# A four-layer graph network: dense columns that are nodes, and ScalarE's one-hots in the tensor pass

## The chip, the cores and the metric

One core of a Trainium2 chip runs the whole network as one program. Time is device microseconds (us) of that core. Engines are called PE (TensorE; PEld its weight loads), DVE (VectorE), ACT (ScalarE), POOL (GpSimd) and SP (SyncE).

## The reference

A graph of 6,250 nodes with 128 features and 100,000 edges. Sources are uniform; the destination is floor(6250 × u²), with the edges sorted by destination, so early nodes have very many edges and late ones few. Four layers run over the same edges, each added to x and normalised:

```python
dst = minimum((6250 * uniform(100000) ** 2.0).astype(int32), 99999); sort src, dst by dst
# layer 0, tensor product
w = silu(edge_attr_10 @ W_fc1 / sqrt(10)) @ W_fc2 / sqrt(100)      # per edge, 10 -> 100 -> 128
agg = segment_sum(concat(w1*y0[src]*ea0, w4*dot(y1[src], ea1), ..., w3*y1[src]*ea0), dst)   # 256 wide
# layer 1, gate and GRU
att = sigmoid(x[src] @ W_att[:d] + x[dst] @ W_att[d:] + b_att)
agg = segment_sum((x[src] @ W_msg + b_msg) * att, dst)
# layer 2, twice: the first four edges of each node, sorted by value, weighted
# layer 3, four SAGE layers, 128 -> 256 -> 256 -> 256 -> 128
mean = segment_sum(z[src], dst) / maximum(count(dst), 1);  z = relu(bn(mean @ Wl.T + bl + z @ Wr.T))
```

## The kernel before

**Edges, tiles, groups.** The sorted edges are cut into tiles of 128 (784 with the padding) and groups of four tiles (196). A pass over *cold* edges gathers the source rows of each tile from a table in DRAM by an indirect DMA that GpSimd issues (L1124, L1333, L1664, some 1.0 us each), makes a one-hot of each edge's place in its group's 128-node window, and TensorE multiplies rows by one-hot and sums the group (L1203, L1452, L1751). VectorE adds the group's sum onto the output at the window's base.

**Hot edges.** Where many edges share a destination, gathers are spared: a *dense* matrix of counts (source by column) is multiplied by the table, 49 blocks of 128 sources. It lies in DRAM as `dense` (49, 128, 3840) in f16. Before the change a column is a place in a narrow *window* of up to 30 nodes: 147 windows cover tiles 0 to 535, one after the other in the columns (`EDGES`), with a base node each (`hot_bases`). After the products VectorE adds each window's columns onto the output at its base (L1847 in the SAGE passes), and in the one-output SAGE passes copies 1/count from node order to window order. The gate pass uses the first 1,792 columns (376 tiles, 94 groups, so 102 cold groups), the two-output SAGE passes 2,304 columns (105 hot groups, 91 cold), the one-output ones 3,840 (134 hot, 62 cold). Columns are worked through in two halves (`supers`) of 49 block steps each.

**Building the counts.** `LateBuild` makes them while other passes gather: for each tile VectorE writes a one-hot of the source's low seven bits and one of the key (source block and place in the window), TensorE multiplies the two and sums a window's tiles in PSUM (L2461), and ScalarE evicts each window (L2479) to its fixed columns in a stage of 256, which SP stores. The first 69 windows are built beside the tensor pass, the rest beside the two sort phases. Tile t of the build is done in the turns of the groups of the pass beside it.

**Prep** (11 to 26 us) makes on VectorE, for every edge, its place in the group's window (`rel`), its key in the dense window, and `far.missed`: 1 where an edge of a dense tile does not lie in its dense window though `rel` is below 128. From the maxima of places over all edges comes one flag:

```python
most = max(max place over its window's width + 128, max rel of dense tiles + 64, max rel of all)
far.any = most > 127.5        # in effect
```

**Far edges.** After each of the six passes `far_pass` (L2006) covers the edges that no window holds. Every engine reads the flag and branches over two loops if it is 0 (L2043 and after): one over 48 windows of 128 nodes, one over the pass's hot groups, in which only the missed edges (`far.missed`) count; the tensor pass has only the first. A turn of a loop is this, on all five engines, and SP starts a turn only when the one before is `done`:

```python
            if eng.If(far.any):
                for w in 1..WINDOWS-1: body(w, first group of the window, w * WIN, False)
                if not tensor: for g in 0..hot_groups-1: body(g + WINDOWS, g, bases[g + 1], True)
```

SP loads 4 × 128 source indices; GpSimd issues four gathers; VectorE makes the one-hots (in the gate pass the slots' operands too, and ScalarE the sigmoids; in the tensor pass the products of the edges); TensorE sums them, twelve 128-column bf16 products for each output of a SAGE pass (rows split in three parts), f32 products in the others; VectorE scales and adds onto the output.

**Tensor pass.** In each group's turn VectorE makes the 512-column f32 one-hot (L1225, is_equal of `iota` and `rel`), the build's one-hots and the products of the edges; ScalarE makes silu and three or four scalings of the gathered rows (L1154) and evicts windows; the hidden layer and two sets of sums are on TensorE.

**Gate pass.** 98 dense steps, one in each of the first 98 cold groups: TensorE makes the block's gate logits (L1424), ScalarE the sigmoids, VectorE the products with the counts (L1503), TensorE the sums. x at the dense columns is taken window by window with the windows' bases. Beside each of the first 94 cold groups one hot group's slot places (the first four edges of a node, for the sort) are worked in, in one pair of small operations.

## Time and profile before

| | |
|---|---|
| time, median of 3 runs | 4,715.51 us (4,713.63 to 4,729.36) |
| the profiled execution | 4,711.36 us, span 4,709.5 us |
| PE busy | 3,546.9 us, 75% (weight loads 2,502.4, 53%) |
| DVE busy | 2,819.4 us, 60% |
| ACT busy | 1,252.7 us, 27% |
| POOL busy | 3,057.2 us, 65% |
| mean granted TensorE clock | 0.858 of full speed |

The stages, in us from the span's start: prep 11 to 26; the first table 30 to 90; tensor pass 94 to 1,183; gate pass 1,272 to 1,895.5; its far pass and the GRU to 1,966; the two sort phases 2,020 to 2,287 and 2,322 to 2,588; four SAGE passes, 2,664.7 to 3,064.9 (one output), 3,165.4 to 3,656.6 and 3,733.2 to 4,223.9 (two outputs), 4,284.5 to 4,669.8 (one output); the end at 4,709.5. Shares of busy time over the whole span mix these; read each stage by itself, in the views that cut the span.

### The profile page before, as it was taken

Reading aid. Unit: us, or ns where it says so; the run is one execution under the profiler, and the core shown is the slowest. Engines: PE = TensorE matmul, PEld = TensorE weight load, DVE = VectorE, ACT = ScalarE, POOL = GpSimd, SP = SyncE. Lnnn points to the kernel's source line nnn. Section 1 sums busy time; section 2 is a strip of 40 time slices with the busy share of each in tenths; the row PEclk is TensorE's granted clock in tenths of the full one; section 3 lists DMA queues with packets and bytes.
Section 4 is the critical chain, followed back from the end, with each engine's and each line's share of the span. In section 5 each row is a group of like instructions: output and inputs, shape, how many; then the busy total and the mean of one; then the engine's idle time right before and its main releaser. Section 6 shows DMA issues by size and latency. Waiting matters only on the chain. (4 is left out here: it accounts for less than half of the span.)

```text
span 4709.5 us, 73302 instructions
## 1 busy us (share of the span) xinstructions
PE 3546.9 (75%) x24179; PEld 2502.4 (53%) x24180; DVE 2819.4 (60%) x8637; ACT 1252.7 (27%) x2796; POOL 3057.2 (65%) x2999
## 2 busy tenths in 40 slices
PE   3788887777777777556445598679998699967894
PEld 2666666666644544333222464447766576755552
DVE  4898888887466666677677534354444535354334
ACT  2333344444244343334333200020000200002112
POOL 3777777777277576367477575537776577746663
PEclk7899999998899898765555799889999899988996
DMA  5222333334233343033333586438886488856872
GB/s 194 66 69 64 94 93 93 91 92 140 73 99 100 81 102 78 18 83 105 90 102 82 197 261 199 149 116 267 265 256 198 164 262 264 261 179 216 247 225 81
DMA packets 432943, 684.60 MB, mean 145 GB/s; under 512 B 66971, under 2 KB 306501, under 8 KB 431801
## 3 DMA queue, kind: packets, MB, share of 16 engines
q1 hardware_dynamic: 311992, 385.14, 25.5%
q0 software_dynamic: 120576, 294.77, 22.7%
q8 instruction: 198, 3.24, 0.3%
q14 instruction: 177, 1.44, 0.1%
HBM read 577.20 MB, written 102.45 MB: 144 GB/s over the span
## 5 line engine op out<-in xcount | busy, mean ns | idle before, releaser
L1664 POOL DMA_INDIRECT pass_rows<-table_sage,src_idx x1216 | 1175.8, 967 | 476.7 <-issue 350.3
L1124 POOL DMA_INDIRECT pass_rows<-table_tensor,src_idx x784 | 834.4, 1064 | 246.8 <-issue 236.8
L1725 PE MATMUL pass_dense_ps<-x 128*128 128x512 f16 (+3 forms) x3528 | 605.8, 327 | 31.8 <-DMA x<-table_sage 30.7
L1333 POOL DMA_INDIRECT pass_rows<-table_gate,src_idx x406 | 433.7, 1068 | 202.3 <-issue 118.2
L1725 PE MATMUL pass_dense_ps<-rb 128*128 128x512 f16 (+1 forms) x2352 | 508.7, 373 | 27.4 <-DMA rb<-table_sage 25.2
L2528 POOL DMA_INDIRECT sort_rows<-table_sort,slot_idx x392 | 396.5, 1012 | 182.1 <-issue 162.3
L1751 PE MATMUL pass_sums_ps<-pass_hot,pass_rows 128*128 128x128 bf16 x5856 | 394.7, 224 | 85.9 <-issue 85.9
L1725 PEld LDWEIGHTS pass_dense_ps<-x 128*128 128x128 bf16 x3528 | 314.4, 98 | 266.6 <-DMA x<-table_sage 31.9
L1751 PEld LDWEIGHTS pass_sums_ps<-pass_hot,pass_rows 128*128 128x128 bf16 x5856 | 367.3, 101 | 108.2 <-issue 92.3
L1786 DVE TENSOR_TENSOR pass_scaled_sums<-pass_sums_ps,rc 128x128 f32<-128x128 f32 x364 | 88.9, 285 | 479.4 <-PE pass_sums_ps L1751 471.6
L1725 PEld LDWEIGHTS pass_dense_ps<-rb 128*128 128x128 bf16 x2352 | 229.2, 100 | 263.6 <-DMA rb<-table_sage 26.3
L1154 ACT ACTIVATE pass_y_ea<-pass_rows,rd 128x128 f32<-128x128 f32 x784 | 250.0, 391 | 405.8 <-DMA pass_rows<-table_tensor,src_idx 405.7
L2461 PE MATMUL sort_counts_ps<-sort_hot_key,sort_hot_low 128*128 128x512 bf16 (+4 forms) x502 | 190.8, 519 | 194.2 <-DVE sort_hot_key L2447 150.5
L1203 PE MATMUL pass_sums_ps<-pass_hot,pass_prod_a 128*128 128x128 f32 x1568 | 234.9, 297 | 131.8 <-DVE pass_prod_b L1015 131.0
L1203 PEld LDWEIGHTS pass_sums_ps<-pass_hot,pass_prod_a 128*128 128x128 f32 x1568 | 209.7, 206 | 186.7 <-issue 177.8
L2461 PE MATMUL pass_counts_ps<-rc 128*128 128x512 bf16 (+8 forms) x1039 | 238.1, 355 | 88.5 <-ACT re L2479 88.5
L1424 PE MATMUL pass_dense_ps<-pass_weighted,rd 128*128 128x512 f32 (+1 forms) x392 | 191.8, 616 | 113.2 <-DVE pass_weighted L1503 110.7
L1786 DVE TENSOR_TENSOR rb<-pass_sums_ps,rc 128x128 f32<-128x128 f32 x124 | 36.0, 290 | 350.6 <-PE pass_sums_ps L1751 334.1
L1203 PE MATMUL pass_sums_ps<-pass_hot,pass_prod_b 128*128 128x128 f32 x1568 | 228.9, 294 | 0.0
L1182 PE MATMUL pass_weight_ps<-fc,pass_hidden 100*128 100x128 f32 x1576 | 221.5, 286 | 1.5 <-ACT pass_hidden L1141 1.0
L1203 PEld LDWEIGHTS pass_sums_ps<-pass_hot,pass_prod_b 128*128 128x128 f32 x1568 | 212.8, 211 | 0.0
L2461 PEld LDWEIGHTS sort_counts_ps<-sort_hot_key,sort_hot_low 128*128 128x128 bf16 x502 | 52.9, 124 | 293.8 <-issue 192.5
(351 smaller groups left out, 6758.1 us busy)
## 6 DMA issues: line engine op xcount, KB each, us to landing
rb<-dense SPq DMA_DIRECT2D x196, 480.0 KB
x<-dense SPq DMA_DIRECT2D x196, 288.0 KB
x<-table_sage SPq DMA_DIRECT2D x196, 192.0 KB
dense<-re SPq DMA_DIRECT2D x11, 3136.0 KB, 13.7
pass_counts<-dense SPq DMA_DIRECT2D x98, 224.0 KB
pass_rows<-table_sage,src_idx POOLq DMA_INDIRECT x1216
rb<-table_sage SPq DMA_DIRECT2D x196, 96.0 KB
table_sage<-x SPq DMA_DIRECT2D x24, 768.0 KB
```

The lines of the kernel that those rows point to most:

```text
L1124: nc.gpsimd.indirect_dma_start(rows[:, h, t, :], None, table, bass.IndirectOffsetOnAxis(ap=idx[:, at:at + 1], axis=0)).then_inc(gathered[h ...
L1154: ins = nc.scalar.activation(y_ea0[:, r, t, :], rows[:, h, t, :], ACT.Copy, scale=cols(extra["edge_attr"], (q * GROUP_TILES + t) * 4, 1))
L1182: ins = nc.tensor.matmul(weight_ps[:, r, t * P:(t + 1) * P], hidden[:, r, t * P:(t + 1) * P], extra["w_fc2"], start=True, stop=True)
L1203: ins = nc.tensor.matmul(sums[:, r, a * WIN:(a + 1) * WIN], prod[:, r, t, :], hot[:, r, t, :], start=(t == 0), stop=(t == GROUP_TILES - 1))
L1333: nc.gpsimd.indirect_dma_start(rows[:, h, t, :], None, table, bass.IndirectOffsetOnAxis(ap=idx[:, at:at + 1], axis=0)).then_inc(gathered[h ...
L1424: ins = nc.tensor.matmul(dense_ps[:, at:to], messages[:, k, 0:P], weighted[:, n % 2, at:to], start=(b == 0), stop=(b == BLOCKS - 1))
L1664: nc.gpsimd.indirect_dma_start(rows[:, h, t, :], None, table, bass.IndirectOffsetOnAxis(ap=idx[:, at:at + 1], axis=0)).then_inc(gathered[h ...
L1725: ins = nc.tensor.matmul(dense_ps[:, at:to], table_ring[:, k, from_table:from_table + P], counts_ring[:, k, at - first:to - first], start= ...
L1751: ins = nc.tensor.matmul(sums[:, r, a * P:(a + 1) * P], rows[:, h, t, at:at + P], hot[:, r, t, :], start=(t == 0 and part == 0), stop=(t = ...
L1786: ins = nc.vector.tensor_tensor(scaled_sums[:, a, :], sums[:, r, a * P:(a + 1) * P], cols(inv_count, start, WIN), ALU.mult)
L2461: ins = self.nc.tensor.matmul(self.counts[:, at:at + wide], self.hot_low[:, (t // G) % 2, t % G, :], self.hot_key[:, r, at:at + wide], sta ...
L2528: nc.gpsimd.indirect_dma_start(rows[:, b, j, :], None, table, bass.IndirectOffsetOnAxis(ap=slot_idx[:, at:at + 1], axis=0)).then_inc(gathe ...
```

## The change

**Columns as nodes.** A dense column is now a node. The near share (tiles 0 to 443, 111 groups) has 2,048 columns for nodes 0 to 2,047; the late share (tiles 444 to 551) has 1,184 for nodes 1,980 to 3,163. Each share is an array of its own. Windows remain as units of the build (126 near and 54 late ones, 180 for 147), and neighbours may overlap: the base of a window is worked out in prep on the chip, as the least of where its tiles' edges begin and the farthest that the windows before it let it begin, each at most its width less one on from the one before, and not below the share's first node. An edge outside its window is missed. The maximum that sets `far.any` is now that of `far.missed` × 128 and of `rel`.

**Build.** The last column of a window may also be the first of the next: TensorE adds to the next window's counts what stands at its first column in the stage (one more product of 49 columns for each window, `same` the identity), and ScalarE evicts at an offset read from a register; keys are ordered place by block. Stages that hold no whole window before them are cleared on ScalarE first. There are eleven stores of the near share for seven, and seven of the late one for eight. Count tiles built beside the tensor pass are 444 for 376, and beside the sorts 42 and 66 for 86 and 74.

**Passes.** The gate pass has 85 cold groups for 102 and 2,048 columns for 1,792: 98 steps now fall in 83 groups, so 15 groups have two; x at the columns is one product of 512 for each bank, with no bases; the 111 hot groups' slots go beside 85 cold ones, so 26 of these have a third unit. Its messages are added in two operations of 1,024 columns. The two-output SAGE passes have 2,048 columns for 2,304 and 85 cold groups for 91. The one-output ones have 2,048 and then 1,184 for 3,840, and 58 cold groups for 62; the windows' adds and the copies of 1/count are gone, one scaling and one add of 2,048 or 1,184 columns stand in their place.

**Tensor pass.** ScalarE makes the one-hots: |rel − iota| per tile (four operations), and then Relu(1 − that) over the group's 512 columns, one group ahead. VectorE's is_equal is gone.

**Sizes.** `far_pass` runs over 111 hot groups in the gate and the two-output SAGE passes and 138 in the one-output ones, if it runs.

The diff, cut to its core:

```diff
-    return 2 * math.ceil((nodes * (1 + 3.5 / math.sqrt(P * (end - first))) + 1) / 2)
...
-NARROW = 30
...
+    return 2 * math.ceil((nodes * (1 + 3.5 / math.sqrt(P * (end - first))) + 2) / 2)
...
+def windows_of(first, end, narrow):
+
+
+    best = {first: (0, [])}
+    for to in range(first + 1, end + 1):
+        best[to] = min((best[a][0] + room_for(a, to) * (to - a + 2) + 50, best[a][1] + [to])
+                       for a in range(max(first, to - MOST_TILES), to) if a in best and room_for(a, to) <= narrow)
+    ends = best[end][1]
+    return ends, [room_for(a, b) for a, b in zip([first] + ends, ends)]
...
+HOT_TILES, DENSE_TILES = 444, 552
...
+NEAR_NODES, LATE_FROM, LATE_TO = 2048, 1980, 3164
+LATE_COLS = LATE_TO - LATE_FROM
+NEAR_ENDS, NEAR_WIDTHS = windows_of(0, HOT_TILES, 30)
+LATE_ENDS, LATE_WIDTHS = windows_of(HOT_TILES, DENSE_TILES, 34)
+HOT_CUTS, WIDTHS = [0] + NEAR_ENDS + LATE_ENDS, NEAR_WIDTHS + LATE_WIDTHS
+GATE_WINDOWS, DENSE_WINDOWS = len(NEAR_WIDTHS), len(WIDTHS)
+NEAR_RUNS = runs_of(range(GATE_WINDOWS), NEAR_NODES)
+LATE_RUNS = runs_of(range(GATE_WINDOWS, DENSE_WINDOWS), LATE_TO)
+LATE_PARTS = ((0, len(LATE_RUNS) // 2), (len(LATE_RUNS) // 2, len(LATE_RUNS)))
+
+SHARES = ((0, HOT_TILES, 0, NEAR_NODES, range(GATE_WINDOWS), NEAR_RUNS),
+          (HOT_TILES, DENSE_TILES, LATE_FROM, LATE_TO, range(GATE_WINDOWS, DENSE_WINDOWS), LATE_RUNS))
+APART = 1 << 15
...
+SUPER_COLS = NEAR_NODES // SUPERS
...
+def window_limits():
+
+
+    rooms, least = [], []
+    for share, (_, _, node, end_node, windows, runs) in enumerate(SHARES):
+        last = runs[-1][0]
+        before = list(itertools.accumulate((WIDTHS[w] - 1 for w in windows), initial=0))
+        reaching = [end_node - STAGE_COLS - max(before[last - windows[0]] - at, 0) for at in before[:-1]]
+        assert reaching[0] <= node
+        rooms += [share * APART + at for at in before[:-1]]
+        least += [max(node, at) for at in reaching]
+    return rooms, least
...
+            def one_hots(q):
+
+
+                if q >= 2:
+                    act.wait_ge(summed, q - 1)
+                    act.wait_ge(hot_made, q - 1)
+                for t in range(GROUP_TILES):
+                    ins = nc.scalar.activation(apart[:, q % 2, t, :], iota[:], ACT.Abs, scale=-1.0,
+                                               bias=cols(rel, q * GROUP_TILES + t, 1))
+                ins.then_inc(apart_made, 1)
+                act.wait_ge(apart_made, q + 1)
+                nc.scalar.activation(hot[:, q % 2, :, :], apart[:, q % 2, :, :], ACT.Relu, scale=-1.0,
+                                     bias=extra["ones"]).then_inc(hot_made, 1)
...
+                    if q + 1 < GROUPS:
+                        one_hots(q + 1)
...
-                nc.vector.tensor_tensor(hot[:, r, :, :], iota[:].unsqueeze(1).broadcast_to([P, GROUP_TILES, WIN]),
-                                        cols(rel, q * GROUP_TILES, GROUP_TILES).unsqueeze(2).broadcast_to([P, GROUP_TILES, WIN]),
-                                        ALU.is_equal).then_inc(hot_made, 1)
...
+    steps_in = spread_over([1] * STEPS, COLD_GROUPS - 2) + [[], []]
+    last_group = [next(j for j in range(COLD_GROUPS) if BLOCKS * (u + 1) - 1 in steps_in[j]) for u in range(SUPERS)]
+    own_in = [[i for i in range(BLOCKS) if 1 + i * (COLD_GROUPS - 2) // BLOCKS == j] for j in range(COLD_GROUPS)]
+    single = [j for j in range(COLD_GROUPS) if len(steps_in[j]) < 2]
+    apart = {single[k * len(single) // len(UNPAIRED)]: g for k, g in enumerate(UNPAIRED)}
...
-                starts = []
-                for part in in_parts(supers[u], 8):
-                    starts = load_bases(PE_E, hot_bases, part[0], len(part))
-                    for w, start in zip(part, starts):
-                        first, end = EDGES[w] - u * SUPER_COLS, EDGES[w + 1] - u * SUPER_COLS
-                        bank = min(end, (first // 512 + 1) * 512)
-                        ins = nc.tensor.matmul(gate_ps[:, first:bank], extra["w_dst"], cols(x, start, bank - first),
-                                               start=True, stop=True)
-                        if bank < end:
-                            ins = nc.tensor.matmul(gate_ps[:, bank:end], extra["w_dst"],
-                                                   cols(x, start + (bank - first), end - bank), start=True, stop=True)
+                for at in range(0, SUPER_COLS, 512):
+                    ins = nc.tensor.matmul(gate_ps[:, at:at + 512], extra["w_dst"], cols(x, u * SUPER_COLS + at, 512),
+                                           start=True, stop=True)
...
+                for c, g in enumerate(beside(j)):
+                    nc.vector.tensor_tensor(hot_narrow[:, r, c, :, :], iota_half[:, 0:HOT_WIN].unsqueeze(1).broadcast_to([P, G, HOT_WIN]),
+                                            hot_rel_half[:, g * G:(g + 1) * G].unsqueeze(2).broadcast_to([P, G, HOT_WIN]),
                                             ALU.is_equal)
...
+                into = agg[:, u * SUPER_COLS:(u + 1) * SUPER_COLS]
+                nc.vector.tensor_tensor(into, into, kept if u == 0 else dense_ps[:, 0:SUPER_COLS], ALU.add).then_inc(dense_added, 1)
+                dve.wait_ge(dense_added, u + 1)
...
+                        for at in range(0, nodes, 512):
+                            to = min(at + 512, nodes)
+                            ins = nc.tensor.matmul(dense_ps[:, a * most_cols + at:a * most_cols + to],
+                                                   table_ring[:, k, from_table:from_table + P], counts_ring[:, k, at:to],
+                                                   start=(b == 0 and part == 0), stop=(b == BLOCKS - 1 and part == PARTS - 1))
                 ins.then_inc(stepped, 1)
...
-                    ins = nc.vector.tensor_copy(inv_dense[:, first:end], cols(inv_count, start, end - first))
-                ins.then_inc(spread, 1)
...
+                    into = aggs[a][:, node:node + nodes]
+                    nc.vector.tensor_tensor(into, into, kept[:, a * most_cols:a * most_cols + nodes],
+                                            ALU.add).then_inc(dense_added, 1)
+                    last_add[a] = (dense_added, u * A + a + 1)
...
+            after(nc.vector.tensor_tensor(under, hot_base, hot_room, ALU.subtract))
+            for share, (first, end, node, _, _, _) in enumerate(SHARES):
+                nc.vector.tensor_tensor(repeated[:, first + MOST_TILES:end], dst[:, first + MOST_TILES:end],
+                                        dst[:, first:end - MOST_TILES], ALU.is_equal)
+                ins = nc.vector.tensor_scalar(least_of[0][:, first:end], under[:, first:end], float(node - share * APART), None,
+                                              ALU.min)
+            after(ins)
+
+            reach, now = 1, 0
+            while reach < DENSE_TILES:
+                nc.vector.tensor_copy(least_of[1 - now][:, 0:reach], least_of[now][:, 0:reach])
+                after(nc.vector.tensor_tensor(least_of[1 - now][:, reach:], least_of[now][:, reach:],
+                                              least_of[now][:, 0:DENSE_TILES - reach], ALU.min))
+                reach, now = 2 * reach, 1 - now
+            after(nc.vector.tensor_tensor(under, least_of[now][:], hot_room, ALU.add))
+            after(nc.vector.tensor_tensor(based, under, hot_least, ALU.max))
...
+            after(nc.vector.tensor_tensor(place, dst[:, 0:DENSE_TILES], based, ALU.subtract))
...
+            after(nc.vector.tensor_tensor(over, place, hot_width, ALU.subtract))
...
+            after(nc.vector.tensor_tensor(least_of[0][:], over, under, ALU.max))
+            for first, end, _, node, _, _ in SHARES:
+                ins = nc.vector.scalar_tensor_tensor(least_of[1][:, first:end], dst[:, first:end], float(-node),
+                                                     least_of[0][:, first:end], ALU.add, ALU.max)
+            after(ins)
+
+            after(nc.vector.scalar_tensor_tensor(over, repeated, -1.0, least_of[1][:], ALU.add, ALU.max))
+            after(nc.vector.scalar_tensor_tensor(inside, over, -0.5, close, ALU.is_le, ALU.mult))
...
+            after(nc.vector.tensor_tensor(far.missed[:], near, inside, ALU.subtract))
...
+            after(nc.vector.reduce_max(most_missed[:], far.missed[:], mybir.AxisListType.X))
+            after(nc.vector.scalar_tensor_tensor(most[:], most_missed[:], float(WIN), most_rel[:], ALU.mult, ALU.max))
...
+        if ends and w > self.windows[0]:
+
+            stage = self.staged(self.run_of(w - 1) % len(self.stages))
+            offset = self.position(PE_E, HOT_CUTS[w], STAGE_COLS - 1)
+            self.nc.tensor.matmul(self.counts[:, 0:BLOCKS], self.same,
+                                  stage[:, :, bass.ds(offset, 1)].rearrange("p b d -> p (b d)"),
+                                  start=False, stop=False, skip_group_check=True)
...
+        stage = self.staged(q % n)
+        if w == first and self.empties(q):
+            self.nc.scalar.activation(stage, self.iota[:, 0:STAGE_COLS].unsqueeze(1).broadcast_to([P, BLOCKS, STAGE_COLS]),
+                                      ACT.Copy, scale=0.0).then_inc(self.emptied, 1)
+            act.wait_ge(self.emptied, sum(map(self.empties, range(self.part[0], q + 1))))
+        if w > self.first:
+            act.wait_ge(self.evicted, w - self.first)
+        at = self.position(ACT_E, HOT_CUTS[w], STAGE_COLS - wide) if w > first else 0
+        self.nc.scalar.activation(stage[:, :, bass.ds(at, wide)],
+                                  self.counts[:, 0:BLOCKS * wide].rearrange("p (d b) -> p b d", b=BLOCKS),
                                   ACT.Copy).then_inc(self.evicted, 1)
...
+                if len(aggs) == 2:
+                    hot_tiles, supers = HOT_TILES, [(dense[0], u * SUPER_COLS, SUPER_COLS, u * SUPER_COLS) for u in range(SUPERS)]
+                else:
+                    hot_tiles, supers = DENSE_TILES, [(dense[0], 0, NEAR_NODES, 0), (dense[1], 0, LATE_COLS, LATE_FROM)]
+                sage_pass(nc, gathers, f"pass3{k}", tab, width, hot_tiles, supers, src_idx, rel, iota_half, bases, room, aggs, own, C)
+                far_edges(f"pass3{k}_far", "sum", tab, width, hot_tiles // GROUP_TILES, aggs, inv_count=C)
...
+    o["hot_width"] = np.repeat(np.asarray(WIDTHS, f32) - 1, np.diff(HOT_CUTS))[None, :]
+    rooms, least = window_limits()
+    o["hot_room"], o["hot_least"] = (np.repeat(np.asarray(v, f32), np.diff(HOT_CUTS))[None, :] for v in (rooms, least))
```

## Rows read from the trace of the kernel before

**Rows 1.** Stretches by stage: start:end, length, busy us by engine, clock, DMA

```profile
94.00:1183.10 1089.10, 860.25 (x5949) 701.08 (x5949) 924.44 (x2626) 434.26 (x1051) 834.37 (x784) 0.93 0.33 89
1272.00:1895.50 623.50, 449.33 (x2532) 306.88 (x2532) 396.05 (x1177) 239.29 (x608) 433.68 (x406) 0.88 0.36 90
...
2664.70:3064.90 400.20, 330.00 (x2214) 200.19 (x2214) 147.63 (x581) 17.99 (x49) 240.20 (x246) 0.90 0.69 214
3165.40:3656.60 491.20, 462.18 (x4340) 332.03 (x4340) 213.03 (x819) 43.01 (x98) 348.18 (x362) 0.97 0.77 244
...
4284.50:4669.80 385.30, 317.03 (x2116) 188.61 (x2116) 139.35 (x532) 42.99 (x98) 237.41 (x246) 0.90 0.69 214
```

**Rows 2.** Groups of instructions, whole span: busy us, mean ns, idle before and releasers

```profile
L1664 POOL DMA_INDIRECT pass_rows<-table_sage,src_idx x1216 | 1175.8, 967 | 476.7 <-issue 350.3 <-PE pass_sums_ps L1751 104.6 <-POOLq L201 21.7
L1124 POOL DMA_INDIRECT pass_rows<-table_tensor,src_idx x784 | 834.4, 1064 | 246.8 <-issue 236.8 <-PE pass_sums_ps L1203 5.7 <-POOLq L201 4.3
L1725 PE MATMUL pass_dense_ps<-x 128*128 128x512 f16 (+3 forms) x3528 | 605.8, 327 | 31.8 <-DMA x<-table_sage 30.7 <-DVE x L1833 1.1
L1725 PE MATMUL pass_dense_ps<-rb 128*128 128x512 f16 (+1 forms) x2352 | 508.7, 373 | 27.4 <-DMA rb<-table_sage 25.2 <-DVE pass_kept L1833 2.2
L1333 POOL DMA_INDIRECT pass_rows<-table_gate,src_idx x406 | 433.7, 1068 | 202.3 <-issue 118.2 <-PE pass_sums_ps L1452 44.5 <-POOLq L201 39.6
...
L1751 PE MATMUL pass_sums_ps<-pass_hot,pass_rows 128*128 128x128 bf16 x5856 | 394.7, 224 | 85.9 <-issue 85.9
...
L1225 DVE TENSOR_TENSOR pass_hot<-iota,rel 128x512 f32<-128x512 f32 x196 | 133.4, 681 | 4.9 <-issue 4.8
...
L1503 DVE TENSOR_TENSOR pass_weighted<-pass_counts,pass_gate_ps 128x896 f32<-128x896 f16 x98 | 105.8, 1079 | 32.1 <-issue 16.4 <-ACT pass_gate_ps L1349 15.6
...
L2479 ACT ACTIVATE re<-pass_counts_ps 128x1470 f16<-128x1470 f32 (+7 forms) x69 | 84.8, 1228 | 137.3 <-PE pass_counts_ps L2461 116.1 <-DMA dense<-re 21.1
```

**Rows 3.** Waits in the first SAGE pass (2664.7 to 3064.9): us, times, longest

```profile
PE pass_own_ps L1707 <- DVE re L1803: 37.4, 6, 12.0
...
PE pass_sums_ps L1751 <- issue: 18.3, 5, 10.5
```

**Rows 4.** Groups of instructions again, VectorE in the SAGE passes

```profile
L1786 DVE TENSOR_TENSOR pass_scaled_sums<-pass_sums_ps,rc 128x128 f32<-128x128 f32 x364 | 88.9, 285 | 479.4 <-PE pass_sums_ps L1751 471.6 <-issue 7.3
...
L1847 DVE TENSOR_TENSOR ra<-ra,pass_kept 128x26 f32 (+9 forms) x294 | 55.0, 187 | 76.0 <-issue 38.2 <-DVE ra L1847 1.3 <-DVE ra L1806 0.3
```

**Rows 5.** Line 2044, sequencers: duration ns min/median/max, first and last start

```profile
L2044 SPq TENSOR_LOAD <-far_any x6: 275/278/466, 1183.6 to 4670.3; - x6
...
L2044 SPq COMPARE_BRANCH  x6: 50/50/50, 1184.4 to 4670.9; - x6
...
L2044 PEldq COMPARE_BRANCH  x6: 200/285/359, 1184.5 to 4671.1; - x6
```

**Rows 6.** DMA issues: times, KB each, median us to landing

```profile
sort_rows<-table_sort,slot_idx POOLq DMA_INDIRECT x392, 2.6
...
sage_early<-in_a_enc SPq DMA_DIRECT2D x1, 64.0 KB, 1.8
```

**Rows 7.** Timeline of the tensor pass around 707 us

```profile
706.22 0.94 POOL L1124 DMA_INDIRECT pass_rows<-table_tensor,src_idx  x1 [0.30 <-issue]
...
708.78 0.98 ACT L1154 ACTIVATE pass_y_ea<-pass_rows,rd 128x128 f32<-128x128 f32 x3 [2.83 <-DMA pass_rows<-table_tensor,src_idx]
```

**Rows 8.** Timeline of TensorE at the gate pass's start

```profile
1292.92 3.36 PE L1424 MATMUL pass_dense_ps<-pass_weighted,rd 128*128 128x512 f32 x4 [3.94 <-DVE pass_weighted L1503]
1296.07 1.20 PE L1445 MATMUL pass_sums_ps<-pass_hot_sig,pass_rows 128*128 128x128 f32 x8
...
1298.40 1.67 PE L1424 MATMUL pass_dense_ps<-pass_weighted,rd 128*128 128x512 f32 x4
```

**Rows 9.** Page, DMA queues of the instruction fetch: packets, MB, share

```profile
q8 instruction: 198, 3.24, 0.3%
q14 instruction: 177, 1.44, 0.1%
```

493 lines of the change are left out of this document (234 added, 259 removed).

## The prediction

> **What bounds the kernel now.** I first read the table of stages [rows 1]. Of each I asked which engine never rests. In the tensor pass it is GpSimd: 784 indirect gathers of 1.064 us, with 0.30 us between two of them that no releaser explains [rows 2], are 784 × 1.37 = 1,071 of 1,089 us. It waited for TensorE only 5.7 us. The gate pass takes longer than its 406 gathers (434 of 623.5 us); there GpSimd waits 44.5 us for TensorE [rows 2], and the loop runs over ScalarE's gates, VectorE's products and TensorE. In the four SAGE passes TensorE is the bound: busy 462 of 491 us with two outputs, 330 of 400 and 317 of 385 us with one. The one-output passes lose the rest where TensorE waits for VectorE's own term (37.4 us in the first) or for something unnamed (18.3 us), in gaps up to 12 us [rows 3]; VectorE is then adding (or copying) windows at 187 ns each, after register loads ("issue", 38.2 us) [rows 4].
>
> One stage hardly appears: the far edges. Six times each engine reads `far_any` and branches past the loops, a load of about 0.3 us and a branch of 0.05 (TensorE's 0.29) [rows 5]. Nothing of line 2043 onward runs but that: the flag is 0.
>
> **The flag after the change.** This decides the case, and it follows from the inputs and the new constants, not from a price. The late share has tiles 444 to 551. Its columns must start at node 1980, so the change clamps the base of its first window to 1980, however late its edges start. The next window may begin at most width − 1 further on. `windows_of` gives the first late windows two tiles and a width of 26, of which 25 places are used: 1980 to 2004, 2005 to 2029, 2030 to 2054. But the expected node at tile 444 is 6,250 × (444 × 128 / 100,000)² = 2,018.7, and two tiles there hold about 18 nodes. The first window holds its edges only if tile 444 starts at or before some 1,986. The fraction 0.568 of 100,000 draws has a deviation of 0.0016, times 2 × 6,250 × 0.568 that is 11 nodes: 1,986 is three deviations away. With the seed of the inputs tile 444 starts at node 2001. Tile 445 then holds nodes 2008 to 2019 against a limit of 2004. Following the new code's bases through all 552 tiles, 298 edges of tiles 444, 445, 447 and 449 lie outside their window; from tile 450 on the bases have caught up, and the near share misses none. Each is marked in `far.missed`, the maximum becomes 1 × 128, and `far.any` is set. Before the change no edge misses (the greatest place is one under its width), in agreement with [rows 5].
>
> **What the flag costs.** All six far stages then run their loops, which cover the missed edges and so keep the sum whole. The loop over windows has 48 turns; all but the tensor pass's add one turn for each hot group: 111, or 138 in the one-output SAGE passes. That is 48 (tensor), 159 (gate), 2 × 159 and 2 × 186 (SAGE): 897 turns. Nothing in a turn is double-buffered: SP waits for `done` of the turn before. One turn, in chain:
> - the index load: a load of 64 KB took 1.8 us, a gather 2.6 from its issue on [rows 6]; I take 2.0.
> - four gathers on GpSimd: 4 × (0.967 + 0.305) = 5.1 us [rows 2].
> - the last one's landing: GpSimd's issue ended at 706.22 + 0.94 = 707.16, ScalarE began on the rows at 708.78 [rows 7]: 1.6 us.
> - TensorE after some 8 us of rest. Four 512-column products took 3.36 us after 3.94 us of idleness and 1.67 us when it had been busy [rows 8], a factor of two, the two levels of its clock. A bf16 product is 394.7 / 5,856 = 0.067 us at the high one [rows 2]; twelve (one output) take 1.6 us at the low one, 24 take 3.2. Eight f32 ones (2 × 0.9 us for each four in [rows 8]) take 3.6.
> - VectorE's scaling and adding, 0.29 us each [rows 4]: 0.7 us, 1.1 with two outputs. In the gate also four sigmoids on ScalarE (1.2, as three operations take 0.98 in [rows 7]) and a 512-column product (0.7, as the one-hot's 0.681 in [rows 2]); in the tensor pass some 2.9 of products, which is what VectorE's 924 / 196 = 4.7 us for each group [rows 1] leaves when the one-hot and the counts' one-hots are off.
> - handovers, four to six at 0.1: 0.4 to 0.6.
>
> Sums: SAGE with one output 2.0 + 5.1 + 1.6 + 1.6 + 0.7 + 0.4 = 11.4; two outputs 13.4; gate 2.0 + 5.1 + 1.6 + 1.2 + 0.7 + 3.6 + 0.6 + 0.5 = 15.3; tensor 16.2. The one-hots, the slot operands and the tensor pass's hidden layer are made while the gathers run (under 5 us against 8.7), so they cost nothing; if they did not fit, each turn would grow by the excess. Total: 372 × 11.4 + 318 × 13.4 + 159 × 15.3 + 48 × 16.2 = 4,241 + 4,261 + 2,433 + 778 = 11,713 us.
> Bounds: with TensorE at the high level throughout, 1,180 us less; with a landing of 2.6 instead of 1.6 (the gather's whole time, [rows 6]), 900 more.
>
> **The rest of the change, against the profiled 4,711.4 us** (span 4,709.5; the median of the runs shown is 4,715.5, 0.1% more).
> - SAGE, two outputs: 98 steps of 3 × 2,048 columns in place of 3 × 2,304 take 606 / 2 × 1/9 = 34 us off TensorE, six groups fewer 6 × 1.56 = 9. The last groups get dense steps too, so its idle time falls a little; GpSimd's 338 × 1.27 + start and end = 440 is then nearly the bound. 491 becomes 446: −45, twice.
> - SAGE, one output: (2,048 + 1,184) / 3,840 leaves 84% of 255 us (−40), four groups fewer −4. The 147 copies and 147 adds per pass become two scalings and two adds of over 1,000 columns, so most of the 56 us of waits in [rows 3] goes. 400 becomes 312 and 385 becomes 305, near GpSimd's 230 × 1.27 = 292. Together −168.
> - Tensor pass: VectorE loses 196 × 0.68 = 133 us [rows 2], but GpSimd sets the pace. ScalarE gains four 128-column operations (1.3 us by [rows 7]) and one of 512 (some 0.6), 1.9 × 196 = 370, and 57 evictions of 1.2 (L2479 in [rows 2]): 434 + 370 + 70 = 874 of 1,089 us, hidden behind the gathers. Matmuls of the counts stay (1,064 for 1,039, and 125 small ones). 0, between −20 (a less busy VectorE beside the gathers) and +60 (TensorE waits at 126 window ends in place of 69).
> - Gate pass: 17 groups fewer × 5.6 ((623.5 − 52) / 102, the 52 an estimate for start, window products and end) = −96; 1/7 more columns in 98 products of 1.079 us [rows 2] +15; 15 groups with two steps at 2.5 (a product and the sigmoids it waits for) +38, and 26 with a third slot unit at 2.4 (seven small operations and a register load) +62; the 138 window products and 69 adds go, −35. −16, between −60 and +30.
> - Prep: some 25 more dependent operations on 552 columns at about 0.7 (the 512-column 0.681): +20. Sort: 52 fewer tiles of counts to build, −8, an estimate, as GpSimd's gathers pace those stages too.
>
> Sum −261: 4,450 us without the loops. With them 4,450 + 11,713 = 16,163, said as 16,160 us.
>
> **Rivals.**
> 1. *The flag stays 0* (I misread a base or the clamp). Then the time is the sum above, 4,450, and this is the side on which it ends faster; it needs that no one of 100,000 edges lies outside its window. For it speaks only that the loops did not run before. Against it stands the arithmetic. 0.11.
> 2. *Every turn fetches its code again.* Each turn jumps back on all five engines. The page's instruction queues moved 3.24 + 1.44 = 4.68 MB for 73,302 instructions, 64 bytes each [rows 9]: the loops that ran before were not fetched twice. But their bodies are other ones, and the one branch over them took TensorE 285 ns against 50 for SP [rows 5]. One fetch of 2.0 us on the chain of each turn would add 897 × 2.0 = 1,800: 18,000 us. 0.07.
> The Trainium skill (Runtime: NRT & Kernel Launch, Instruction fetch mechanics) says that a taken branch whose target isn't in the present window of two pages makes the engine fetch it before it goes on; by that these short bodies would be spared, and the forecast stands, and if they straddle pages it is this rival. The bytes of [rows 9] agree with the first reading.
> 3. *Cheaper turns*: TensorE stays at the high level and handovers vanish: 11,713 − 1,180 − 450 → 14,500 us. 0.05, inside the range.
>
> **Numbers.** 0.75 for the forecast, 0.05, 0.07 and 0.11 for the rivals, 0.02 for something else (of which half within the 0.3% that a measurement of this kernel can tell from no change). Slower 0.88, same 0.01, faster 0.11. The range runs from rival 3 with 900 us to spare, 13,600, to rival 2 with the longer landing, 18,900. It leaves out mainly rival 1; if that held, its own range would be 4,370 to 4,560.
>
> **What would show it.** Right: the far lines (L2043 onward before the change) with hundreds of gathers each, 897 × 4 = 3,588 gathers more, turns of 11 to 16 us, TensorE's clock at 0.5 there, and SAGE passes of about 446 and 310 us beside them. Wrong: six branches as in [rows 5] and a span under 4,600; or turns whose longest wait is none of the five above.

## The result, and the profile after

The changed kernel takes 16,751.2 us (median of 4 runs, 16,737.3 to 16,757.8) against 4,720.7 of the kernel before on the same chip: a ratio of 3.548 (3.540 to 3.555). The profiled execution has a span of 16,755.9 us. The forecast was 16,160, in a range of 13,600 to 18,900.

Stretches by stage, as in [rows 1] (start:end, length, busy us of PE, PEld, DVE, ACT and POOL, clock, DMA share, GB/s); every second one of these lines is a far pass, which [rows 5] showed as a branch:

```profile
114.40:1435.30 1320.90, 871.43 (x6099) 715.28 (x6099) 818.02 (x2515) 869.90 (x2090) 801.17 (x784) 0.86 0.42 83
1437.70:2243.80 806.10, 370.30 (x1248) 269.12 (x1248) 234.58 (x672) 89.98 (x240) 181.03 (x192) 0.54 0.07 17
2328.90:2856.20 527.30, 405.00 (x2230) 247.57 (x2230) 384.03 (x1111) 230.24 (x540) 367.89 (x338) 0.93 0.42 104
2856.80:5526.80 2670.00, 934.09 (x2862) 467.61 (x2862) 548.25 (x1751) 182.09 (x636) 599.96 (x636) 0.50 0.08 16
6340.20:6642.70 302.50, 279.71 (x2019) 172.47 (x2019) 101.98 (x277) 18.02 (x49) 226.79 (x230) 0.97 0.82 252
6645.00:8788.80 2143.80, 271.77 (x2232) 222.72 (x2232) 422.28 (x1116) 0.00 (x0) 702.90 (x744) 0.50 0.14 34
8889.10:9330.40 441.30, 417.87 (x3608) 277.87 (x3608) 170.30 (x532) 42.97 (x98) 327.68 (x338) 0.98 0.81 254
9332.80:11503.80 2171.00, 435.85 (x3816) 393.91 (x3816) 424.86 (x1272) 0.00 (x0) 600.90 (x636) 0.54 0.21 58
...
14257.70:14561.80 304.10, 270.18 (x1921) 161.11 (x1921) 93.65 (x228) 43.01 (x98) 228.13 (x230) 0.98 0.79 240
14564.10:16716.20 2152.10, 271.78 (x2232) 222.71 (x2232) 422.29 (x1116) 0.00 (x0) 714.24 (x744) 0.50 0.13 34
```

(In the order of the lines: tensor pass, its far pass, gate pass, its far pass, first SAGE pass and its far pass, second and its far pass, fourth and its far pass.) The flag is set. The six far passes, with the third SAGE pass's 2,179 us, are 806 + 2,670 + 2,144 + 2,171 + 2,179 + 2,152 = 12,122 us. In them the clock is 0.50 to 0.54, the lower of the two levels nearly throughout, and no engine is busy for half of a stretch. Without them 16,756 - 12,122 = 4,634 us remain.

The gathers of the far loops, line by line of the code (duration min/median/max, first and last start):

```profile
L2114 POOL DMA_INDIRECT pass_far_rows<-table_sage,pass_far_idx x2760: 940/946/1192, 6647.7 to 16711.2; - x198
L2114 POOL DMA_INDIRECT pass_far_rows<-table_gate,pass_far_idx x636: 938/944/999, 2861.0 to 5516.6; - x159
L2114 POOL DMA_INDIRECT pass_far_rows<-table_tensor,pass_far_idx x192: 938/944/952, 1440.5 to 2234.0; - x192
```

2,760 + 636 + 192 = 3,588, which is four for each of 897 turns: as forecast, to one.

One turn of the first SAGE far pass, from the add that ends the turn before to the one that ends this:

```profile
7001.99 0.29 DVE L2245 TENSOR_TENSOR ra<-ra,pass_far_scaled_sums 128x128 f32 x1
...
7005.02 0.94 POOL L2114 DMA_INDIRECT pass_far_rows<-table_sage,pass_far_idx  x1 [6.83 <-DMA pass_far_idx<-in_src]
...
7008.77 0.95 POOL L2114 DMA_INDIRECT pass_far_rows<-table_sage,pass_far_idx  x1 [0.30 <-issue]
...
7011.52 1.46 PE L2168 MATMUL pass_far_sums_ps<-pass_far_hot,pass_far_rows 128*128 128x128 bf16 x12 [10.09 <-DMA pass_far_rows<-table_sage,pass_far_idx]
7013.12 0.29 DVE L2238 TENSOR_TENSOR pass_far_scaled_sums<-pass_far_sums_ps,rc 128x128 f32<-128x128 f32 x1 [8.19 <-PE pass_far_sums_ps L2168]
7013.54 0.29 DVE L2245 TENSOR_TENSOR ra<-ra,pass_far_scaled_sums 128x128 f32 x1
```

It is one serial chain: nothing of the next turn has begun before this one ends, and VectorE's one-hots (not shown) lie under the index load. 2.74 us pass from the end of the add (7,002.28) to the first gather, for handing over, loading 2 KB of indices (4 × 128 of 4 bytes) and handing over again; four gathers take 4.70; 1.80 until TensorE has the last rows; its twelve products 1.46 at the low clock; 0.14, and 0.71 for scaling and adding. Together 11.55 us, the time from one add to the next; the passes' mean is 2,143.8 / 186 = 11.53.

Next the instruction fetch, with 140,036 instructions run (packets, MB, share):

```profile
q8 instruction: 182, 2.98, 0.1%
q14 instruction: 169, 1.38, 0.0%
```

The changed kernel with the flag clear (experiment 1), which skips every loop and runs 68,170 instructions, fetched the same 182 and 169 packets, 4.36 MB. That settles rival 2: no turn fetched its code again. The Trainium skill (Runtime: NRT & Kernel Launch, Instruction fetch mechanics) lets a taken branch force a fetch only where its target lies outside the present window of two pages; the bytes agree.

**What went the other way.** The prediction had the tensor pass at 1,089 us still. It took 1,321. Waits there (us, times, longest):

```profile
POOL pass_rows L1141 <- PE pass_sums_ps L1237: 272.9, 42, 36.5
...
ACT re L2550 <- DMA dense<-re: 202.1, 9, 24.8
...
ACT re L2544 <- DMA dense<-re: 26.4, 1, 26.4
```

ScalarE waits 202.1 + 26.4 = 228 us for the store of the stage of counts to land; before it was 21.1 us in four waits. The issues of this store, before and after (KB, median us from issue to landing, over the whole span):

```profile
dense<-re SPq DMA_DIRECT2D x11, 3136.0 KB, 13.7
```

```profile
dense<-re SPq DMA_DIRECT2D x14, 3136.0 KB, 27.2
```

The same 3,136 KB in one store, at twice the time. One such wait on ScalarE, and on GpSimd at the same time:

```profile
772.46 0.72 ACT L1171 ACTIVATE pass_hot<-rd,ones 128x512 f32<-128x512 f32 x1
797.96 1.07 ACT L2550 ACTIVATE re<-pass_counts_ps 128x1078 f16<-128x1078 f32 x1 [24.78 <-DMA dense<-re]
```

```profile
783.61 0.94 POOL L1141 DMA_INDIRECT pass_rows<-table_tensor,src_idx  x1 [0.31 <-issue]
807.27 0.94 POOL L1141 DMA_INDIRECT pass_rows<-table_tensor,src_idx  x1 [22.71 <-PE pass_sums_ps L1237]
```

ScalarE stands before the first eviction of a run. Behind it in its queue are the hidden layer and the scaled rows of the next group; without them TensorE makes no sums and no buffer of rows comes free. GpSimd, which sets the pace, ends its last free gather at 784.6 us and then stands for 22.7.

### The profile page after: what moved, and what is told of

Same layout as the page of the kernel before. It is cut to its first block and busy times, and to the rows that moved or that the text cites. A ratio compares the mean times of both kernels' runs of the same rounds, so it can differ in the third digit from the quotient of the medians.

```text
span 16755.9 us, 140036 instructions
## 1 busy us (share of the span) xinstructions
PE 6005.4 (36%) x38254; PEld 4255.4 (25%) x38255; DVE 4988.6 (30%) x14480; ACT 1959.6 (12%) x4622; POOL 6297.6 (38%) x6439
## 5 line engine op out<-in xcount | busy, mean ns | idle before, releaser
L2114 POOL DMA_INDIRECT pass_far_rows<-table_sage,pass_far_idx x2760 | 2619.0, 949 | 6045.5 <-DMA pass_far_idx<-in_src 5311.9
L2168 PE MATMUL pass_far_sums_ps<-pass_far_hot,pass_far_rows 128*128 128x128 bf16 x12096 | 1415.2, 312 | 7240.2 <-DMA pass_far_rows<-table_sage,pass_far_idx 7240.2
L2168 PEld LDWEIGHTS pass_far_sums_ps<-pass_far_hot,pass_far_rows 128*128 128x128 bf16 x12096 | 1233.2, 146 | 7422.2 <-DMA pass_far_rows<-table_sage,pass_far_idx 7422.2
L2114 POOL DMA_INDIRECT pass_far_rows<-table_gate,pass_far_idx x636 | 600.0, 943 | 2080.5 <-DMA pass_far_idx<-in_src 1907.9
L2171 PE MATMUL pass_far_sums_ps<-pass_far_hot_sig,pass_far_rows 128*128 128x128 f32 x1272 | 506.6, 502 | 1615.7 <-DVE pass_far_hot_sig L2216 1615.7
L2200 DVE TENSOR_TENSOR pass_far_match<-iota,pass_far_moved 128x512 f32<-128x512 f32 x897 | 621.1, 692 | 30.8
L2203 DVE TENSOR_TENSOR pass_far_hot<-pass_far_match,pass_far_past 128x512 bf16<-128x512 f32 (+1 forms) x897 | 620.7, 692 | 30.6
L1757 PE MATMUL pass_dense_ps<-x 128*128 128x512 f16 x2352 | 539.5, 381 | 30.7 <-DMA x<-table_sage 30.5
L1757 PE MATMUL pass_dense_ps<-rb 128*128 128x512 f16 x2058 | 423.7, 360 | 25.6 <-DMA rb<-table_sage 24.0
L2172 PE MATMUL pass_far_slot_ps<-pass_far_hot,pass_far_slot_in 128*9 128x128 f32 x1272 | 379.7, 402 | 0.0
## 6 DMA issues: line engine op xcount, KB each, us to landing
dense<-re SPq DMA_DIRECT2D x14, 3136.0 KB, 27.2
```

The costliest lines, as they stand in the source:

```text
L1757: ins = nc.tensor.matmul(dense_ps[:, a * most_cols + at:a * most_cols + to], table_ring[:, k, from_table:from_table + P], counts_ring[:, k ...
L2114: nc.gpsimd.indirect_dma_start(rows[:, t, :], None, table, bass.IndirectOffsetOnAxis(ap=idx[:, t:t + 1], axis=0)).then_inc(far.gathered, 16)
L2168: ins = nc.tensor.matmul(sums[a][:, 0:WIN], rows[:, t, at:at + P], hot[:, t, :], start=(first and part == 0), stop=(last and part == PARTS ...
L2171: nc.tensor.matmul(sums[0][:, 0:WIN], rows[:, t, 0:P], hot_sig[:, t, :], start=first, stop=last)
L2172: ins = nc.tensor.matmul(slot_ps[0:SLOT_ROWS, 0:WIN], slot_in[:, t, :], hot[:, t, :], start=first, stop=last)
L2200: nc.vector.tensor_tensor(match[:], iota[:].unsqueeze(1).broadcast_to(shape), moved[:].unsqueeze(2).broadcast_to(shape), ALU.is_equal).the ...
```

## The experiments

Ratios are to the kernel before, with 95% intervals; its median was 4,709 to 4,715 us in these sets. Every variant named a_ but a_one_gather has the edit of experiment 1 as well, and the diffs are cut to their core.

**1. The flag undone by one constant** (a_from2000). The late share's columns start where its first window still reaches the edges.

```diff
-NEAR_NODES, LATE_FROM, LATE_TO = 2048, 1980, 3164
+NEAR_NODES, LATE_FROM, LATE_TO = 2048, 2000, 3164
```

> The changed kernel with one constant altered: the late share's columns start at node 2000 (1,164 columns) instead of 1980, so that the first late window reaches past tile 444's edges. By the new bases no edge is missed then. Theory 1 (the flag and its six far passes are the whole slowdown): the six far passes shrink from 12,122 us to six branches, and the time is 16,756 - 12,122 = 4,634, give or take 15. Rival (part of the slowdown lies elsewhere, or the loops also run for another reason): far loops still in the trace, or a time away from 4,634 by over 50. The tensor pass should stay at 1,321 us, as it is before the first far pass.

4,587.0 us, 0.974 (0.972 to 0.976); no far line in the trace. The whole slowdown was the flag, set by 298 edges of 100,000; with it clear, the change makes the kernel 2.6% faster. Its stages (tensor, gate, first, second and fourth SAGE pass):

```profile
112.60:1399.70 1287.10, 854.28 (x6014) 703.06 (x6099) 816.96 (x2515) 868.44 (x2090) 802.58 (x784) 0.88 0.40 85
1491.90:2020.40 528.50, 405.37 (x2230) 247.40 (x2230) 384.20 (x1111) 229.85 (x540) 369.04 (x338) 0.93 0.41 104
2823.50:3124.60 301.10, 277.62 (x2019) 171.01 (x2019) 101.90 (x277) 17.99 (x49) 225.69 (x230) 0.97 0.82 253
3224.40:3665.40 441.00, 417.93 (x3608) 277.40 (x3608) 170.18 (x532) 42.97 (x98) 327.51 (x338) 0.98 0.81 254
4242.90:4541.50 298.60, 268.82 (x1921) 159.56 (x1921) 93.45 (x228) 43.02 (x98) 223.81 (x230) 0.99 0.80 244
```

It is 47 us faster than 4,634: the tensor pass took 1,287 and not 1,321, and two stretches after the sort phases 4 and 8 us less; the stores took 24.4 us and not 27.2. That needn't be the edit's doing: a_one_gather (experiment 3) has the code of the changed kernel up to the first SAGE far pass, flag set, and its tensor pass took 1,280 us with stores at 23.2. So some 40 us in this pass lie between two kernels with the same code up to there; why, stays open.

**2. The flag alone** (b_forced): the kernel before, made to run its loops over nothing.

```diff
-            nc.vector.tensor_scalar(far.any[:], top[:], float(WIN), None, ALU.is_ge)
+            nc.vector.tensor_scalar(far.any[:], top[:], 0.0, None, ALU.is_ge)
```

> The kernel before with its flag set whatever the data are, so that the six far passes run though no edge is missed (they add nothing). If a turn's price is the same in both kernels and the loops don't depend on how many edges are missed: 48 turns at 16.8 us (tensor), 142 at 16.8 (gate), 364 at 11.55 and 306 at 13.67 (SAGE) = 11,580 us more, 16,290 in all. Rival (the price comes with the change or the missed edges): away from it by over 300.

16,260 us, 3.450 (3.440 to 3.460), 30 from the forecast: the loops' price is a number of turns, and neither the missed edges nor the rest of the change has a part in it that can be seen.

**3. What a turn is made of** (a_one_gather): one gather for four in the SAGE far loops, whose sums are then wrong.

```diff
-                for t in range(T):
+                for t in range(1 if plain else T):
                     nc.gpsimd.indirect_dma_start(
...
-                    pe.wait_ge(far.gathered, w * (16 * T) + before)
+                    pe.wait_ge(far.gathered, w * 16 + before)
...
-                                ins = nc.tensor.matmul(sums[a][:, 0:WIN], rows[:, t, at:at + P], hot[:, t, :],
+                                ins = nc.tensor.matmul(sums[a][:, 0:WIN], rows[:, 0, at:at + P], hot[:, t, :],
```

> The changed kernel (columns from 1980, flag set), but in the SAGE passes' far loops a turn gathers one tile's rows instead of four, and all four products read those; the sums there are then wrong. The prediction put the gathers in the chain of each turn: 690 turns lose 3 x 1.25 us, 2,588 in all, so 16,751 - 2,588 = 14,163. Rival (the transfers' latency or another engine holds the turn, and the gathers run beside it): over 15,000.

13,959 us, 2,792 less (forecast 2,588). The far passes after the first and second SAGE pass:

```profile
6570.10:7978.00 1407.90, 271.77 (x2232) 222.70 (x2232) 421.76 (x1116) 0.00 (x0) 175.99 (x186) 0.50 0.06 13
8520.20:10068.10 1547.90, 435.83 (x3816) 393.89 (x3816) 424.14 (x1272) 0.00 (x0) 150.20 (x159) 0.54 0.08 20
```

1,407.9 / 186 = 7.57 us per turn, 3.96 less; 1,547.9 / 159 = 9.74, 3.9 less. Three gathers are 3.75 of that; the last 0.2 is a landing and an index load of some 0.1 less each (1.66 us to TensorE for 1.80, 2.61 to 2.67 to the first gather for 2.74). TensorE's and VectorE's busy times are those of the changed kernel to 0.2%, so it is the gathers that left the chain. The loops lost some 2,720 us; the other 73 are gone before the first SAGE pass, where the code is the same.

**4. One-hots on ScalarE, alone** (b_act_hots): the diff's `one_hots`, its calls and the removed is_equal, put into the kernel before.

> The kernel before with one part of the change alone: the tensor pass's one-hots from ScalarE (four |rel - iota| and one Relu per group), VectorE's is_equal gone. The prediction's term says 0, hidden behind GpSimd's gathers: 4,715 +- 15, pass 1,089. Rival (ScalarE's chain of silu, scalings, one-hots and evictions, in order, is too near the gathers' pace once it has waited for a store): pass 1,110 to 1,150 and 4,740 to 4,780.

4,688.5 us, 0.9953 (0.994 to 0.9967): 0.5% faster, outside both ranges. The pass fell from 1,089 to 1,063.5 us. Its groups:

```profile
L1126 POOL DMA_INDIRECT pass_rows<-table_tensor,src_idx x784 | 799.1, 1019 | 251.8 <-issue 235.6 <-PE pass_sums_ps L1222 12.3 <-POOLq L201 3.9
...
L1152 ACT ACTIVATE rd<-iota,rel 128x128 f32<-128x128 f32 x784 | 248.9, 388 | 73.1 <-PE pass_sums_ps L1222 73.1
...
L1156 ACT ACTIVATE pass_hot<-rd,ones 128x512 f32<-128x512 f32 x196 | 141.5, 722 | 6.3
```

784 gathers at 1,019 ns instead of 1,064 [rows 2]: 35 us less busy on GpSimd, with nothing of its own changed. VectorE's 133 us of is_equal went, and 390 us of ScalarE's operations (388 and 722 ns) came in their place, so the gathers are the slower beside the former.

**5. One-hots back on VectorE in the changed kernel** (a_dve_hots; the reverse edit, on top of experiment 1).

> As a_from2000, and VectorE makes the tensor pass's one-hots again with one is_equal per group. In the changed kernel the pass took 1,321 us against 1,089, and ScalarE waited 228 us for the stores of the count stages. Theory A (the stores' landing alone sets the loss, 10 waits of some 23 us): the pass stays within 20 us of 1,321 and the total of 4,634. Theory B (ScalarE's extra 390 us slow each group to some 5.9 us, so that GpSimd can't win back in between what a stall cost): the pass falls to 1,180 to 1,230, the total to 4,500 to 4,540.

4,594.3 us, 0.976 (0.974 to 0.978), the pass at 1,297 and not 1,287. Theory B fell: ScalarE's one-hots don't make the loss. Theory A is nearer, but its bounds, 20 us about 1,321 and 4,634, were missed by 4 and 20 us, and that the landing alone sets the loss is not shown (experiment 7 speaks against it).

**6. Where a store lands** (a_aligned, a_align64, b_odd_pitch). Three edits of the store's destination and the array's rows. The first two leave the counts in wrong columns, so they are for the time alone:

```diff
 # a_aligned: 512-byte steps                   # a_align64: at = q * 224, rows alike
-    return sum(WIDTHS[w] - 1 for w in SHARES[share][4]) + STAGE_COLS
+    return (3072, 1792)[share]
...
-        at = self.position(SP_E, HOT_CUTS[first] + 1, self.most) if q > 0 else 0
+        at = q * STAGE_COLS
 # b_odd_pitch, in the kernel before
-            dense = dram("dense", (BLOCKS, P, SLIM_COLS), F16)
+            dense = dram("dense", (BLOCKS, P, SLIM_COLS + 1), F16)
```

> As a_from2000, but each stage of counts is stored at a column that is a multiple of 256, in arrays whose rows are a multiple of 512 bytes, instead of at its node's column. The counts then stand in wrong columns; instructions and bytes are the same. Theory (the stores slowed from 13.7 to 27.2 us because their 512-byte rows no longer begin on a 512-byte boundary): stores take some 14 us again, ScalarE's waits for them fall from 228 to under 100 us, the tensor pass to 1,180 to 1,230, and the two stretches after the sort phases lose some 30 us: 4,470 to 4,540 in all. Rival (the stores are slow for what runs beside them): 27 us and 4,634 stay.

> As a_aligned, with the stages stored at multiples of 224 columns (448 bytes: every start on a 64-byte boundary, hardly one on 512 bytes), one over the other by 32 columns. Counts stand in wrong columns again. If 64 bytes are the boundary that matters, stores take some 14 us and the time is that of a_aligned, 4,457. If it is 512 bytes, they take some 25 us and the time is that of a_from2000, 4,587.

> The kernel before with rows of the counts' array one element longer (3,841 instead of 3,840), so that rows begin 7,682 bytes apart; stores and reads move the same bytes. Theory (rows that don't begin on a 512-byte boundary make a stage's store slow): stores take 24 to 27 us instead of 13.7, ScalarE waits some 80 us more for them in the tensor pass, and the time goes up by 50 to 100 us to 4,760 to 4,810. Rival (the boundary doesn't matter; the changed kernel's stores are slow for another reason): 13.7 us and 4,712.

The stores' rows, in that order:

```profile
dense<-re SPq DMA_DIRECT2D x14, 3136.0 KB, 13.6
```

```profile
dense<-re SPq DMA_DIRECT2D x14, 3136.0 KB, 15.3
```

```profile
dense<-re SPq DMA_DIRECT2D x11, 3136.0 KB, 25.3
```

a_aligned: 4,456.7 us, 0.945 (0.944 to 0.947), 130 less than a_from2000, the tensor pass at 1,178. a_align64: 4,464.8, 0.947 (0.945 to 0.950). b_odd_pitch: 4,766.6, 1.012 (1.009 to 1.014), with the kernel before's stores slowed to 25.3 us and its tensor pass from 1,089 to 1,139. So in the tensor pass a store whose 512-byte rows begin at any 2-byte place has a median of 23 to 27 us, in both kernels; one whose rows begin on 64 bytes takes 13.5 (a_whole below) to 15.3, and on 512 bytes 13.6. A start between 2 and 64 bytes wasn't tried by itself. A rival, that a computed address makes the store slow, falls: b_odd_pitch has fixed addresses and is slow, a_whole computed ones and is fast. The place is not all, though: the late share's stores, beside the sorts, took 32 to 45 us in a_from2000 and 25 in b_odd_pitch, and that is not explained. A row of a_from2000's:

```profile
dense<-rd SPq DMA_DIRECT2D x4, 3136.0 KB, 36.8
```

The Trainium skill (DMA: Bandwidth & Descriptors, How a descriptor splits into AXI transactions) names 256 bytes as the boundary off which extra beats are paid. By that a_align64, with 13 of 18 stores off it, should stand near the odd ones; at 15.3 us it stands near the aligned ones, so the measurement decides against that as the main cost here. As a small cost it agrees: the five stores on 256 bytes took 12.9 to 13.8 us, the thirteen others 14.0 to 16.7.

In a_aligned waits remain:

```profile
POOL pass_rows L1141 <- PE pass_sums_ps L1237: 136.5, 43, 23.1
...
ACT re L2550 <- DMA dense<-re: 74.4, 9, 10.8
```

**7. Two half stages** (a_halves), so that evictions needn't wait for a store:

```diff
-STAGE_COLS = 256
+STAGE_COLS = (128, 256)
...
-                                       dense[0], [E], [dense_stored], (build_hot_low, build_hot_key)))
+                                       dense[0], [E[:, 0:NP // 2], E[:, NP // 2:NP]], dense_stored, (build_hot_low, build_hot_key)))
```

> As a_from2000, with two stages of 128 columns for the near share in the room of the one of 256, so that windows are evicted to one while the other is stored: 23 stores of 1,568 KB (rows of 256 bytes) instead of 11 of 3,136. If the waits for the one stage are the loss (192 us), the tensor pass falls from 1,287 to between 1,080 and 1,130, and the total to 4,380 to 4,430. Rival (a store of as many, shorter rows takes as long as the whole one did, and 23 of them slow the gathers): the pass stays over 1,200 and the total over 4,500.

4,514.7 us, 0.958 (0.955 to 0.960); the pass 1,227 us. ScalarE's waits for stores, 192 us in a_from2000, are gone, but only 60 us came back, within the bounds that the rival in the expectation had (over 1,200 and over 4,500):

```profile
PE pass_counts_ps L2526 <- ACT re L2552: 194.1, 69, 13.5
POOL pass_rows L1142 <- PE pass_sums_ps L1238: 191.6, 52, 11.6
```

The transfers got dearer, as that rival has it. Here is the stretch from 915 to 1,115 us (columns as in [rows 1]) in the kernel before and in a_halves:

```profile
915.00:1115.00 200.00, 157.90 (x1106) 127.14 (x1105) 169.15 (x481) 89.30 (x200) 155.07 (x140) 0.93 0.35 95
```

```profile
915.00:1115.00 200.00, 149.27 (x971) 118.15 (x986) 138.17 (x396) 141.75 (x330) 122.67 (x123) 0.91 0.88 98
```

Nearly the same GB/s take 0.88 of the DMA engines' time for 0.35 (0.40 in a_from2000). So this edit takes one cost away and brings another, and what it gains is not the price of the waits alone.

**8. Evictions ahead of the one-hots** (a_halves_order).

```diff
-                    if q + 1 < GROUPS:
-                        one_hots(q + 1)
                     for t in build.turns(q, BUILD_TURNS):
                         for w in build.ended(t):
                             build.evict(act, w)
+                    if q + 1 < GROUPS:
+                        one_hots(q + 1)
```

> As a_halves, with ScalarE's evictions of windows issued ahead of the one-hots of the next group instead of behind them. In a_halves TensorE waits 194 us for evictions, each behind 2 us of one-hots, and GpSimd 192 us for TensorE. If the order on ScalarE makes that wait, the pass falls from 1,227 by 40 to 100 us, the total to 4,415 to 4,475. Rival (evictions are late for the gathers' late landing beside the stores, up to 13.9 us): no change, 4,505 to 4,525.

4,517.5 us, 0.958 (0.956 to 0.961): no change.

```profile
POOL pass_rows L1142 <- PE pass_sums_ps L1238: 183.7, 99, 8.7
...
PE pass_counts_ps L2526 <- ACT re L2552: 122.4, 68, 6.4
```

TensorE's wait for evictions fell by 72 us, GpSimd's for TensorE by 8. So that part of the wait wasn't what held GpSimd. The time lies in the range of the expectation's rival, gathers that land late beside the stores; the DMA share of the pass is still 0.64, against 0.33 in [rows 1].

**9. Aligned stores with the counts in place** (a_whole): prep rounds each run's start down to a multiple of 32, and

```diff
+            self.nc.scalar.activation(stage[:, :, 0:ALIGN], self.staged((q - 1) % n)[:, :, bass.ds(was, ALIGN)],
+                                      ACT.Copy).then_inc(self.emptied, 1)
```

> As a_from2000, with every stage of counts stored at a multiple of 32 columns (64 bytes) in rows of a multiple of 512 bytes, and all counts in their right columns: prep rounds a run's base down to 32, ScalarE first copies 32 columns of the stage before to the head of the next (49 x 32 elements, about 1.3 us), and a run holds 224 columns, so there are 13 and 8 runs in place of 11 and 7. By a_align64's stores of 14 to 15 us, less 130 us and with some 25 us back for the runs, copies and prep: 4,470 to 4,500, tensor pass 1,190 to 1,215. If the copy and the two runs more eat what the faster store gives, it stays above 4,560.

4,520.9 us, 0.960 (0.958 to 0.962): 66 us gained, not 100 and more. Stores take 13.5 us and the stretches after the sorts are those of the kernel before, but the tensor pass is 1,245 us, not 1,200: ScalarE waits 112.8 us in 12 waits for 87.5 in 10 in a_aligned, since 13 shorter runs mean two stops more, and copies heads for 18.1 us. That is 43 of the 66 us between the two passes; the rest is not accounted for.

**10. Both together** (a_both): half stages for the near share, aligned stores for the late one.

> The parts that helped put together: columns of the late share from node 2000, two half stages for the near share and evictions ahead of the one-hots (a_halves_order), and the late share's stages stored at multiples of 32 columns with the head copied (from a_whole). Beside the near share nothing changes against a_halves_order. In a_whole the stretch from the tensor pass's end to the first SAGE pass was 29 us shorter than in a_halves_order, and prep 4 us longer: 4,518 - 25 = 4,493, between 4,480 and 4,505. If the slow stores there were hidden after all, it stays at 4,518.

4,510.7 us, 0.956 (0.954 to 0.959), 17 us above the forecast and 5 above its range; it is the lowest time of a kernel with all counts in place, but its interval overlaps that of a_halves. From the tensor pass's end to the first SAGE pass it gained 39 us for the 29 expected; the tensor pass gave 29 back (1,251 and not 1,222), where, against a_halves_order, only the length of the array's rows differs (2,816 columns for 2,726). That is not explained.

## Why the prediction was right, and where not

**The flag** was right in every step: the clamp at node 1,980, the missed edges, 897 turns, 3,588 gathers; experiment 1 shows that the flag is the whole slowdown, experiment 2 that turns alone make it, without a missed edge.

**The turns**: forecast 11,713 us, measured 12,122, 3.5% more. SAGE with one output 11.53 and 11.57 (11.4 said), two outputs 13.65 and 13.71 (13.4), gate 16.79 (15.3), tensor 16.79 (16.2). Within a SAGE turn errors cancelled, which was luck: the index load with its handovers 2.74 for 2.0, the landing 1.80 for 1.6, the gathers 4.70 for 5.1, since the pause behind the last isn't part of the chain, TensorE 1.46 for 1.6, the other handovers 0.14 for 0.4. The gate turn was mis-sized by 1.5 us on TensorE, 5.09 for 3.6: the eight products for the slots, which the sum left out, lie between the f32 ones of the messages. The 3.6 itself doesn't come out of [rows 8], where eight of these products take 1.20 us at a granted clock of 0.87, so some 2.1 at the low level; in the far turns they took 3.2. In the tensor turn the first gather waits for two loads, 3.14 us after the add and not 2.0.

**Rivals.** The first and second fell (experiment 1, the fetched bytes). Of the third, TensorE stayed at the low level (a mean of 0.50 to 0.54) and the handovers did not vanish.

**The rest of the change** was the weak part: 4,450 forecast without loops, 4,634 in the changed kernel and 4,587 with the flag clear.
- SAGE passes: two outputs 441 and 440 (446 said), one output 303 and 304 (312 and 305). Of the first pass's 98 us, 50 are TensorE's busy time (330 to 280), and the 56 us of waits in [rows 3] are gone from the list, as the prediction had it for the windows' adds and copies.
- Gate: 527 for 607. The -96 is just what the 17 groups fewer were priced at, so the other four terms, +80 in sum, came to nothing. The second steps and third slot units, priced at 38 + 62 us, cannot be seen: VectorE was busy 396 us before and 384 after. Which of the terms was wrong, no run separates.
- Prep: the tensor pass starts 20.4 us later, as said. (A slip in what bounds that pass: 784 × 1.37 is 1,074; the 1,071 is the row's own 834.4 + 236.8. Nothing hangs on it.)
- Sorts: -8 said. From the last gather of the first sort to the first of the second it went from 44.9 to 60.0 us, and from the last of the second to the first of the SAGE passes from 83.8 to 109.0. Each follows a store of the late share: a part of the sort's table is waited for up to 15.3 us (1.3 before) in the one, a weight 15.4 in the other. With aligned stores (a_whole) the two stretches are 47.4 and 84.3 us.
- Tensor pass: **this step failed.** The prediction took the 57 evictions as 1.2 us each on ScalarE, "hidden behind the gathers", within +60 us; it took +232 (+191 and +198 in a_one_gather and a_from2000). It never asked how long the store took that the first eviction of a run waits for. With the destination now a node's column, rows begin at any 2-byte place: 13.7 us became 23 to 27 (experiment 6), with eleven stores and not seven. Nothing hides them: there are 126 windows in the pass for 69, one in some 9 us for one in some 16, and a window of 16 us covered most of a store of 13.7. Aligned placement gives 109 of the 198 back. Where no eviction waits for a store (a_halves), some 138 over 1,089 are still there, and their cause stays open. Moving ScalarE's one-hots away or behind the evictions didn't shorten the pass by more than 5 us (experiments 5 and 8). GpSimd's waits come mostly in the second half of the pass, where a window ends in nearly every group, which would fit the one buffer of counts that TensorE must leave for each of 126 evictions; but experiment 8 took 72 us off TensorE's wait for evictions and next to nothing off the pass. The other candidate is the DMA engines' time, 0.88 for 0.35 late in the pass (experiment 7), with gathers that land late. No run had fewer windows, a second buffer or half stages stored on 64 bytes.
- The ScalarE one-hots are a small gain (-25 us in the kernel before), a little past the bound of -20 that the prediction gave a less busy VectorE.

## What to carry to other kernels

A path that covers rare cases can cost more than everything else: when a change moves the bounds of the usual path, work through the data that sit at its edges before pricing a single instruction. When a transfer's destination becomes a computed place, its time has to be priced anew, since the same bytes took nearly twice as long at 2-byte places as at multiples of 64 bytes; and an engine that waits for one store stops everything behind it in its queue.
